# Two expert loads and the attention's half sums moved in their engines' queues

## What is computed

```
q = xn @ Wq (32 heads of 16); k, v = xn @ Wkv (8 groups of 16)
attn = softmax(causal(q k^T) / 4) v @ Wo + bo
scores = sigmoid(xn @ gate_w.T) + bias;  top 4 of 16 experts, weights normalised
ffn = sum over chosen experts of w * (silu(xn Wg) * (xn Wu)) Wd   (inner width 256)
      + silu(xn Sg.T) * (xn Su.T) @ Sd.T                          (shared expert)
out = x + attn + ffn
```

## Time and profile before

| | us |
|---|---|
| median of 3 runs | 535.72 (535.19 to 537.13) |
| the profiled execution, its time | 536.95 |
| its span in the trace | 535.1 |
| TensorE busy | 462.7 (86%) |
| VectorE busy | 361.4 (68%) |
| ScalarE busy | 283.4 (53%) |
| GpSimd busy | 235.5 (44%) |
| mean granted clock of TensorE | 0.952 |

### The profile page before, as it was taken

One profiled execution on the slowest core, in us unless ns is written; L12 is line 12 of the kernel. 1 busy time (PEld: TensorE's weight loads), 2 busy tenths in 40 slices (PEclk: granted clock), 3 DMA queues, 4 the chain that ended last, 5 costly groups with the idle time before them and its releaser, 6 DMA issues.

```text
span 535.1 us, 9881 instructions
## 1 busy us (share of the span) xinstructions
PE 462.7 (86%) x3074; PEld 345.7 (65%) x3074; DVE 361.4 (68%) x604; ACT 283.4 (53%) x434; POOL 235.5 (44%) x175
## 2 busy tenths in 40 slices
PE   3998959967999998899985989998969999989870
PEld 2867748845776776667663767676747767767640
DVE  7488644785577868938799595489685655965620
ACT  2722221614656776646786647286726546666610
POOL 2111619631444644634338654152566443264321
PEclk9999979998999998999998789998979999999996
DMA  7916962549746547965777766857674423445243
GB/s 275 375 36 153 249 202 70 148 140 213 211 81 159 116 84 236 244 174 122 151 209 205 218 153 116 213 108 169 181 171 73 83 45 60 78 67 96 42 56 43
DMA packets 31878, 77.93 MB, mean 146 GB/s; under 512 B 4048, under 2 KB 11728, under 8 KB 28912
## 3 DMA queue, kind: packets, MB, share of 16 engines
q1 hardware_dynamic: 18864, 45.92, 27.9%
q0 software_dynamic: 11856, 27.27, 27.8%
q10 hardware_dynamic: 1104, 4.06, 3.7%
HBM read 54.04 MB, written 23.07 MB: 144 GB/s over the span
## 4 chain that ended last, share of the span: by engine, by line
PE 48%; DMA 17%; DVE 15%; issue 7%; ACT 5%; SPq 2%; ACTq 1%; POOL 1%; DVEq 1%; POOLq 0%
PE psum L1173 17%; PE psum L1163 9%; DMA out<-ysb,tab 9%; DVE wsplit L986 6%; DMA q_parts<-stage 4%; PE psum L1315 3%; PE psum L1193 2%; PE psum L1126 2%; DVE plo L1028 2%; PE psum L1214 2%; PE psum L1303 2%; PE psum L1198 2%; PE psum L1181 2%; ACT wsplit L627 1%; PE psum L1280 1%
## 5 line engine op out<-in xcount | busy, mean ns | idle before, releaser
L1173 PE MATMUL psum<-wsplit,xgT 128*128 x564 | 163.0, 429 | 17.7 <-DVE wsplit L986 17.7
L488 POOL DMA_INDIRECT out<-ysb,tab x47 | 81.4, 1732 | 158.1 <-ACT ysb L652 91.7
L1173 PEld LDWEIGHTS psum<-wsplit,xgT 128*128 128x128 f32 x564 | 106.3, 202 | 38.7 <-issue 20.6
L1163 PE MATMUL psum<-wsplit,zT 128*128 (+1 forms) x330 | 90.3, 409 | 7.6 <-DVE zT L957 3.5
L971 DVE TENSOR_REDUCE negm<-psum 128x4 f32<-128x512 f32 x64 | 59.6, 954 | 25.1 <-PE psum L1198 25.1
L478 POOL DMA_INDIRECT xg<-xn_rows,tab x47 | 62.9, 1338 | 29.5 <-PE psum L1214 14.3
L1163 PEld LDWEIGHTS psum<-wsplit,zT 128*128 128x128 f32 x330 | 59.3, 189 | 23.5 <-issue 12.5
L652 ACT ACTIVATE ysb<-psum,tab 128x512 f32<-128x512 f32 x47 | 32.3, 687 | 74.5 <-PE psum L1163 69.2
L1028 DVE TENSOR_TENSOR plo<-xn,phi 128x1536 f16<-128x1536 f32 x32 | 59.1, 1847 | 15.0 <-ACT phi L705 12.9
L981 DVE TENSOR_TENSOR xgT<-psum,xgT 128x512 fp32r<-128x512 f32 x47 | 32.3, 688 | 48.4 <-ACT xgT L623 48.0
L699 ACT ACTIVATE xn<-psum 128x1536 f32<-128x1536 f32 x32 | 46.3, 1446 | 23.0 <-PE psum L1288 14.8
(11 more groups left out here) (190 smaller groups left out, 731.7 us busy)
## 6 DMA issues: line engine op xcount, KB each, us to landing
wraw<-wexp SPq DMA_DIRECT2D x17, 1024.0 KB, 6.6
wraw<-wexp SPq DMA_DIRECT2D x17, 512.0 KB, 4.3
q_parts<-stage SPq DMA_DIRECT2D x16, 192.0 KB
xn<-x SPq DMA_DIRECT2D x4, 512.0 KB, 5.2
xn_rows<-xn SPq DMA_DIRECT2D x8, 256.0 KB, 7.8
ctxs<-x SPq DMA_DIRECT2D x8, 256.0 KB, 4.5
out<-ysb SPq DMA_DIRECT2D x8, 256.0 KB, 3.2
out<-xn POOLq DMA_DIRECT2D x8, 256.0 KB, 4.4
```

The source lines that it names most:

```text
L488: nc.gpsimd.indirect_dma_start(out=out, out_offset=rows_of(s), in_=ysb[:, par, :], in_offset=None, compute_op=ALU.add).then_inc(y_out[par] ...
L1163: last = MM(dst, lhs(a, k), split_weights(place, w, c), start=m == 0, stop=m == len(products) - 1)
L1173: last = MM(bank(GUB[par]), xgT[:, par, a, k, :], split_weights(place, w, k * 512), start=k == 0 and a == w == 0, stop=k == KD - 1 and a = ...
```

## The change

SP issues the loads of expert 0 (1.5 MB) no longer ahead of the stores of units 4 and up, but after tile 1 of its loop. Those of expert 1 (1.5 MB) come after tile 3. The two raises of `w_ready` for expert 0 move from t = 0 and 1 to t = 3, between the two loads of expert 1. On GpSimd `add_attention` moves to the head of slots j = 3 and 4, ahead of `add_rows` and `down_low`. The waits that keep the adds apart move by one slot with it: a0 now waits for the scatter of slot 12b and not 12b + 1, a1 for that of slot 12b + 1; the waits for `att_out` stand before the scatters 12b + 1 and 12b + 2. After the last batch nothing changes in order.

```diff
             sp.wait_ge(parts_out[1], units_out(3))
             pack_half(sp, 1, 0)
-            for part, cols in enumerate(PARTS):
-                sp.dma_start(wraw[:, 0, cols], wexp[0, :, cols]).then_inc(we_in[part][0], 16)
-
-            sp.wait_ge(ws_low, len(STEPS))
-            for part, cols in enumerate(PARTS):
-                sp.dma_start(wraw[:, 1, cols], wexp[1, :, cols]).then_inc(we_in[part][1], 16)
-
             for t in range(NT):
                 if EARLY + t < UNITS:
                     store_unit(EARLY + t)
...
                 sp.dma_start(out[t * P:(t + 1) * P, :], ysb[:, t % 2, :]).then_inc(stored[t % 2], 16)
-                if t < 2:
-                    sp.wait_ge(we_in[t][0], 16)
-                    sp.sem_inc(w_ready[t], 1)
+                if t == 1:
+                    for part, cols in enumerate(PARTS):
+                        sp.dma_start(wraw[:, 0, cols], wexp[0, :, cols]).then_inc(we_in[part][0], 16)
+                if t == 3:
+                    sp.wait_ge(ws_low, len(STEPS))
+                    for part, cols in enumerate(PARTS):
+                        sp.dma_start(wraw[:, 1, cols], wexp[1, :, cols]).then_inc(we_in[part][1], 16)
+                        sp.wait_ge(we_in[part][0], 16)
+                        sp.sem_inc(w_ready[part], 1)
...
-                if s > SPS and s % SPS in (2, 3):
-                    pool.wait_ge(att_out, 32 * (s // SPS) + (0 if s % SPS == 2 else 16))
+                if s > SPS and s % SPS in (1, 2):
+                    pool.wait_ge(att_out, 32 * (s // SPS) + (0 if s % SPS == 1 else 16))
...
-                newest = SPS * (b + 1) + 1 + qt if b < B - 1 else NSLOT - 1
+                newest = SPS * (b + 1) + qt if b < B - 1 else NSLOT - 1
...
                             gather(SPS * b + (j + 3), 1 - j % 2, SPS * b + (j + 2))
+                        if b and j in (3, 4):
+                            add_attention(b - 1, j - 3)
                         s = SPS * b + j
...
                         if 0 < s < NSLOT:
                             down_low_of(number)
-                        if b and j in (3, 4):
-                            add_attention(b - 1, j - 3)
```

## The result

The changed kernel took 530.69 us (median of 7 runs, 530.01 to 532.84), the kernel before beside it 535.72. The ratio is 0.9918, with a 95% interval of 0.9890 to 0.9945: faster by 4.4 us (2.9 to 5.9) by the ratio and 5.0 by the medians, where the forecast was 524.2 and its range ended at 530.5. In a second session, beside the experiments, it took 528.69 against 537.16 (0.9895, interval 0.9835 to 0.9956). The medians are of all runs of a kernel and the ratios of its fast runs alone, so the two can differ by a few us.

The account below looks back on a forecast made before the run. The prediction saw TensorE idle behind a late store in the opening and GpSimd's line of adds, each waiting for a landing, in the batches. 7.6 + 3.9 = 11.5 us off 535.72 gave 524.2, range 518 to 530.5.

Parts of the forecast that it names:

- Part 1: Opening: moving the loads of experts 0 and 1 from in front of unit 4's store gains 7.6 us.
- The store was taken to land at 64: Opening: unit 4's store, behind the pack reads alone, lands at 64, between bounds of 63.0 and 69.2.
- The next limiter: Opening: ScalarE's wait for unit 6's own store, ending at 92.57 before, moves by 7.4 us to about 85.2.
- `w_ready` was never waited for: Opening: raised at about 90.2, wanted by ScalarE at 93.2; 3 us of slack, cost nothing.
- Rival (c): Opening: the packs hold unit 4's store, which lands at 69 all the same; about 529, chance 0.09.
- Part 2: Batches: the new order of GpSimd's half sums gains 3.9 us, ends -3 and +14.
- r15 at 267.7 if its landings are like these: Batch 1, GpSimd's line: this scatter, at 271.19 before, comes about 3.5 us earlier.
- holds `ysb`'s buffer for the evacuation two slots on, some 10 us away: Batch 1: r13's added wait for a0 also holds the buffer that a later evacuation needs, some 10 us off.
- I take 2.4, about a third of the gather waits: Batches 1 and 2: gain from TensorE's gather waits (8.3 us); upper bound 12.7, lower bound nothing or a loss.
- Rival (a): Whole kernel: the moved loads gain as worked out, the moved half sums nothing; 528.1, chance 0.23.
- Batch 3: Last batch, where GpSimd's line itself ends the kernel: the new half-sum order gains about 1.5 us.
- Rival (e): Three batches: r13's delay passes into the gather behind it; 8 us slower, 543.7, chance 0.03.

Follow-up runs that it names:

- e1: Changed kernel with GpSimd's half sums put back in the old order, new load order kept: 531.25 us, ratio 0.9906 to the kernel before.
- e2: Kernel before with only GpSimd's new order of the half sums, SP's loads as before: 538.77 us, ratio 1.0026 to the kernel before.
- e10: Kernel before's SP load order, with both half sums issued together at the head of slot j = 3: 530.03 us, ratio 0.9830 to the kernel before.
- e6: Changed kernel with both half sums issued together at the head of slot j = 3: 521.66 us, ratio 0.9693 to the kernel before.
- e7: Changed kernel with a third buffer for `ysb`: 528.03 us, ratio 0.9855 to the kernel before.
- e3: Changed kernel with the old half-sum order and expert 0's load back ahead of unit 4's store: 532.48 us, ratio 0.9900 to the kernel before.
- e8: Changed kernel with both half sums issued together at the old place, behind scatter 12b + 1 and its down_low: 525.33 us, ratio 0.9774 to the kernel before.
- e11: Changed kernel with both half sums issued together at slot j = 3 and a third `ysb` buffer: 520.40 us, ratio 0.9662 to the kernel before.

## Why the prediction was wrong

**Part 1 was right in mechanism, and in size up to the first scatter.** Forecast 7.6 us. The store was taken to land at 64; the evacuation that waits for it came at 65.39, in an execution that had started 0.7 late. TensorE didn't idle and kept its clock, as counted (3.61 us against 5.63). The next limiter, the evacuation of unit 8, was put at 85.2 and came at 85.69. `w_ready` was never waited for. The stores behind expert 1's load cost nothing that reaches r0, which came 7.3 us earlier. Over the whole kernel the part comes out smaller: 5.0 us by e1 (3.0 to 7.1), 5.8 by e2 against the changed kernel, 7.4 by e10 against e6. So 7.6 may be 1 to 3 us too much there; the runs don't say where it would be lost. Rival (c) falls.

**Part 2 was wrong: 3.9 us forecast, none measured (in e2 a cost of 1.4, interval from a gain of 0.7 to a cost of 3.5).** Three steps failed.

- "r15 at 267.7 if its landings are like these": the steps were not like these. I took 5.2 to 5.4 us for each. The changed kernel's steps from r12 on are 6.7, 5.8, 5.8, 4.9 and 7.0 (first rows of batch 1 above). In the kernel before the step from a1 (issued at 264.34) to r15 at 271.19 was already 6.9. The sum was 26.9 and is 30.3, and with the 3.4 us the whole gain of the line is gone. The gap ahead of r13 was filled, as described, but by a longer step: r12 was taken to land 5.4 us after its issue, which no row showed, and a0 could go 6.7 after it. The other long step is there in both kernels, the last one ahead of r15. Both times an expert's weights were loading: the DMA engines moved 264 GB/s in the 6.9 us before and 251 in the 7.0 of the changed kernel, and 68 to 120 in the steps of 4.9 to 5.8 ahead of it. That this traffic is what makes a step long is likely, but no run changed it alone.
- "holds `ysb`'s buffer for the evacuation two slots on, some 10 us away": this was looked up for r13 only. The late one is r26, two adds further down the line, and in batch 2 slots 24 to 28 took 34.0 us from evacuation to evacuation in four traces with the new order there, and 31.8 in four with the old. The buffer is only part of that: e7 takes the wait for it away and wins 0.8 us in this stretch. What holds the rest stays open.
- "I take 2.4, about a third of the gather waits": the gather waits did fall, from 8.3 to 6.0 us, but TensorE's waits for VectorE rose from 17.7 to 18.7. By the means of three traces of each pure order (before, e1, e3; changed twice, e2) it is 8.8 to 7.0 and 17.3 to 19.1: what the one gave back the other took. The forecast named VectorE as the later one in its lower bound and its rivals, and gave it too little weight. Rival (a), nothing from part 2, is the case that came nearest, at 528.1. The median missed it by 2.6 us. Whether that is batch 2's loss or an opening worth 5 us over the whole kernel is open.

Batch 3 was nearly right: 1.5 us forecast, 2.2 won up to r39, 0.9 left at r46. The give-back was not in the sum, which took the line from r39 on as moving in one piece. Rival (e) fell too: the gather of slot 19 was no later against r12 (14.4 us behind it, and 14.3 before).

The range stopped at 530.5, since it held no case in which part 1 was right and part 2 cost something. By e2 a small loss was as near as the gain.

## What to carry to other kernels

Loads that nobody waits for yet don't belong ahead of a store in the same queue that an engine waits for: here 3 MB cost 7.3 us at the first scatter and 5 to 7 over the kernel, and half of it half (3.8 us at the first scatter). In a line of DMAs that each wait for the one before, changing the order moves the waits about, while taking one step out (two adds on disjoint rows issued together) gave 7 us more. Where a line's step is worth something is to be read batch by batch: in batch 2 five of the us won are time at the lower clock level that doesn't occur, and in batch 1, where VectorE's splitting was as late as the gathers, nothing was won. Before a reorder is credited with a gain, the buffers that each later step frees are to be followed down the line, not only those of the step that was moved.

## What the runs showed of the hardware

Two accumulating DMAs of 256 KB each, issued together, let the next one go 6.4 to 9.0 us after the first's issue (e6, e8, e10, e11); one alone took 4.7 to 8.1 (the other traces). For equal bytes the step depends on when it runs. An idle time of TensorE of 1.61 us left the projection behind it at 3.72 us, at a granted clock of 1.00 (e3); behind 5.60 us it took 5.63, at 0.50 from 74 to 78 us. And GpSimd's issue of a gather, 1.0 us as a rule, took 1.6 to 2.4 us in 16 of the 47 gathers of the changed kernel. Each of the 16 began while a VectorE operation on two SBUF inputs was running that had started first, and each ended 0.9 us after that operation did. One of them (changed kernel, two timelines):

```profile
234.65 1.76 DVE L1027 TENSOR_TENSOR plo<-xn,phi 128x1536 f16<-128x1536 f32 x1
```

```profile
235.29 1.98 POOL L477 DMA_INDIRECT xg<-xn_rows,tab  x1 [0.30 <-issue]
```
